# A hybrid network on one core: twelve logarithms of ScalarE moved behind the second head's copies

## What is computed

```python
sim = k @ q_i                                   # causal: -inf beyond query i
_, top_idx = jax.lax.top_k(sim, 8)              # eight keys
for comb in COMBS:                              # all singles, then all pairs of the eight slots
    idx = concat([i], top_idx[slots])           # the query's own key and one or two others
    K = k[idx]; V = v[idx]
    gram = einsum('cnd,cmd->cnm', K, K)
    det = jnp.linalg.det(gram)
    log_det = jnp.log(jnp.where(valid, det, 1.0) + 1e-06)
    score = log_det / float(s + 1)
    w = softmax(einsum('cnd,d->cn', K, q_i) / 4)
    out_s = einsum('cn,cnd->cd', w, V)
probs = softmax(scores)
y = probs @ outs
```

## Time and profile before

| | us |
|---|---|
| median of 3 runs | 6697.57 |
| lowest, highest | 6695.38, 6705.53 |
| profiled execution, its own time | 6691.49 |
| its span, first to last instruction | 6689.8 |

### The profile page before, as it was taken

The page is one execution under the profiler, slowest core; times in us unless marked ns, Lnnn a source line. Parts: engine busy times, 40 slices in busy tenths (PEclk is TensorE's granted clock), DMA queues, the critical chain, the costliest instruction groups (busy, mean ns, idle before and its releaser), DMA issues. The chain is left out here.

```text
span 6689.8 us, 140956 instructions
## 1 busy us (share of the span) xinstructions
PE 4900.3 (73%) x46216; PEld 3823.2 (57%) x46217; DVE 4611.5 (69%) x9872; ACT 2738.6 (41%) x9313; POOL 1463.5 (22%) x1253
## 2 busy tenths in 40 slices
PE   5777776867877777777877788765089498419995
PEld 2333334756666666666666666655078376419995
DVE  5777774328999999999999999994168744312224
ACT  3343342214555555555555555542322133333331
POOL 1323322110000000000000000000645200266663
PEclk8777778987667777767767777765599699559997
DMA  8000000002111111211211111111222500211114
GB/s 144 8 5 7 5 3 6 0 7 78 71 68 70 72 65 72 72 69 69 72 72 66 72 71 66 72 59 29 70 70 75 109 0 10 77 61 46 46 46 138
DMA packets 226734, 370.27 MB, mean 55 GB/s; under 512 B 104818, under 2 KB 187355, under 8 KB 201028
## 3 DMA queue, kind: packets, MB, share of 16 engines
q1 hardware_dynamic: 200036, 309.26, 15.6%
q0 software_dynamic: 26112, 53.64, 2.4%
HBM read 287.04 MB, written 75.78 MB: 54 GB/s over the span
## 5 line engine op out<-in xcount | busy, mean ns | idle before, releaser
L2729 PE MATMUL l2a_g<-l2a_feat,l2a_onehot 128*128 128x33 bf16 x27648 | 782.7, 182 | 357.8 <-DVE l2a_onehot L2600 155.6
L2729 PEld LDWEIGHTS l2a_g<-l2a_feat,l2a_onehot 128*128 128x128 bf16 x27648 | 762.1, 100 | 419.0 <-issue 238.7
L2592 DVE TENSOR_REDUCE l2a_dots<-l2a_prod 128x144 f32<-128x2304 f32 x192 | 489.7, 2551 | 4.5
L1942 PE MATMUL l_y<-l_hc,l_selT 128*96 128x512 f32 x384 | 295.4, 864 | 264.9 <-POOL l_hc L1780 264.3
L2675 PE MATMUL l2a_s<-l2a_qkT 32*128 32x128 f32 (+1 forms) x1536 | 488.2, 453 | 0.0
L2701 PE MATMUL l2a_m<-main_ident,l2a_pv 128*96 128x128 f32 x2304 | 349.6, 326 | 87.7 <-DVEq L2537 87.7
L2365 POOL TENSOR_TENSOR l2a_veto<-l2a_gone 128x288 f32<-128x288 f32 x64 | 42.6, 665 | 1681.5 <-DVE l2a_prod L2585 1681.5
L2600 DVE TENSOR_SCALAR l2a_onehot<-l2a_spread,l2a_pos 128x4096 bf16<-128x4096 bf16 x288 | 361.3, 1283 | 62.3 <-DVE l2a_hd L2498 20.1
L2701 PEld LDWEIGHTS l2a_m<-main_ident,l2a_pv 128*96 128x96 f32 x2304 | 341.6, 207 | 103.5 <-issue 100.2
L1780 POOL TENSOR_TENSOR l_hc<-l_hs,l_bc 128x512 f32<-128x512 f32 x192 | 243.3, 1267 | 716.0 <-DVE l_hs L1847 714.8
L2675 PEld LDWEIGHTS l2a_s<-l2a_qkT 32*128 32x128 f32 x1536 | 310.8, 250 | 86.4 <-issue 38.6
(11 more groups left out here) (412 smaller groups left out, 11615.4 us busy)
## 6 DMA issues: line engine op xcount, KB each, us to landing
l2a_spread<-l2a_idx_rows SPq DMA_DIRECT2D x192, 1024.0 KB, 4.7
rows_in<-main_zeros SPq DMA_DIRECT2D x1, 13824.0 KB, 80.3
l2f_xg<-rows_in SPq DMA_DIRECT2D x72, 192.0 KB
l3f_xg<-rows_in SPq DMA_DIRECT2D x72, 192.0 KB, 2.5
l2f_combine_y<-rows_out SPq DMA_DIRECT2D x32, 384.0 KB, 3.8
l3f_combine_y<-rows_out SPq DMA_DIRECT2D x32, 384.0 KB, 4.7
l3f_w<-in_l3f_w SPq DMA_DIRECT2D x2, 4608.0 KB, 31.6
l_xT<-in_l_xT SPq DMA_DIRECT2D x16, 384.0 KB, 3.8
```

The costliest lines, as they stand in the source:

```text
L1942: nc.tensor.matmul(y_ps[:, :], selT[:, g, :], hc[:, g % 2, :], start=g == 0, stop=g == G - 1).then_inc(hc_used, 1)
L2592: nc.vector.tensor_reduce(dots[:, quad_of(s[2]), 0:NPROD], prod[:, :, :, :], AX.X, ALU.add).then_inc(S["dots_ready"], 1)
L2729: ins = nc.tensor.matmul(o[:, a * FEAT:a * FEAT + 2 * HS + 1], onehot[:, kt, at:at + P], feat3[:, s[1], kt, part, h, 0:2 * HS + 1], start= ...
```

## The change

In ScalarE's `body`, `log_det` no longer stands first. In steps with copies it is called inside the loop over the four heads, behind the copies of the second one (j = 1). Where no copies are due (the drain's last step) it stands where it stood. Nothing else is changed, and line numbers behind it move by 2 (L2315 becomes L2313, L2324 becomes L2326).

```diff
--- before.py
+++ after.py
@@ -2298,8 +2298,6 @@
                 def body(n, u, i, back, last):
                     if i == 0 and u == 1:
                         keep_tables()
-                    if stage(back, LOGS):
-                        log_det(*stage(back, LOGS))
                     s = back(2)
                     if s:
                         q, t = count_of(s), s[2] // QUADS
@@ -2316,6 +2314,10 @@
                             nc.scalar.copy(keys[:, s[2] % 2, j, SLOTS:EXT, :], src[:, 0:EXT - SLOTS, 0:HS])
                             ins = nc.scalar.copy(values[:, t, h, :, :], src[:, :, HS:2 * HS + 1])
                             ins.then_inc(S["kv_ready"], 1)
+                            if j == 1 and stage(back, LOGS):
+                                log_det(*stage(back, LOGS))
+                    elif stage(back, LOGS):
+                        log_det(*stage(back, LOGS))
                     if in_range(n):
                         q = count_of((n, u, i))
                         act.wait_ge(S["scored"], counted(q * 2 + 2))
```

## The result

The changed kernel takes 6743.97 us (median of 4 runs, 6741.58 to 6748.62) against 6696.70 us of the kernel before in the same comparison: a ratio of 1.0069, with a 95% interval of 1.0051 to 1.0086. It is slower by 47 us. The forecast was 6717, or 19.5 us slower, with a range to 6734. The direction was right, but the forecast rise was less than half of the measured one, and the time lies outside the range.

What follows compares the result with a forecast made beforehand. VectorE was taken to set the pace; 23.5 us of added waits for the logarithms less a 4 us gain made 19.5 us, so 6717 us from the median 6697.6. The range was 6698 to 6734.

Steps and rivals of the forecast that it cites:

- What bounds the kernel: In the edited stage VectorE sets the pace, busy 379 of 400 us; TensorE, busy 315, does not.
- the third rival: TensorE sets the pace, so some 60 pauses of 3 us come off, 180 us, giving 6518; chance 0.03.
- Step 3, the logarithms: On ScalarE in step 3, the logarithms start 1.2 us later, behind two heads' copies.
- What VectorE pays, the odd images: At L2494: 13 late places (already waiting) pay 1.2 us more each; touching (slack about 0) 1.17; middle (0.19 to 0.43) the uncovered rest.
- What VectorE pays, the even images: At L2494 in step 3: touching places pay 1.17 us each, middle ones 1.2 less their slack, early ones nothing.
- Early: 9 x 0: Nine early step-3 places, all in even images, cost nothing, since a slack of 1.24 us covers the 1.2 us shift.
- Step 0: Logarithms 0.4 us later in even images, 0.7 in odd; slack of 2.19 or more covers it, costing VectorE nothing.
- Early images turn middle or late: If TensorE's clock falls less well, nine early slacks shrink to 0.4 or 0: 7 to 11 us more; chance 0.12.
- TensorE's pauses count: Same as the third rival: TensorE sets the pace and 180 us of pauses come off, giving 6518; chance 0.03.
- Step 3, the copies: TensorE's pause moves to the wait for ScalarE's cast; its next step is 0.3 us later, costing nothing.
- The small gain: In step 4, GpSimd's squares slow VectorE less in late images: 0.26 us each, some 4 us off.
- What would show it: L2494's waits for logarithms some 38 us in 20 or more waits, about 2.3 us each in late images.

Runs made afterwards that it cites:

- e1: The kernel before, with the logarithms moved behind the second head's copies in step 3 alone: 6704.79 us against 6696.87, ratio 1.0015.
- e2: The kernel before, with the logarithms moved behind the second head's copies in step 0 alone: 6698.50 us, ratio 1.0004.
- e3: The changed kernel, with TensorE's fourth head of step 0's gather held until the logarithms are done: 6714.70 us against 6696.87, ratio 1.0026.

## Why the prediction was wrong in size

*What bounds the kernel: right.* VectorE's work fell, its waits for the logarithms rose by 47.2 us, and the stage by 40.7. Over the twelve kernels VectorE's busy time in the stage stays between 2796 and 2810 us, while its idle time goes from 149 to 212. TensorE's 137.7 us of pauses for copied values went, and brought nothing, as the third rival's chance of 0.03 had it.

*Step 3, the logarithms: right.* The shift was to be 1.2 us and is 1.2.

*What VectorE pays, the odd images: the number came, in part by luck.* Thirteen late, one touching, one middle, at 1.1 + 1.2, 1.17 and about 1.0 make 32 us; the odd images of after wait 32.5. But the forecast ascribed this to step 3's move by itself, and with that alone (e1) they wait 20.1, 6 us more than before and not 18, since their fronts come 0.8 us earlier there, which the forecast didn't have.

*What VectorE pays, the even images: this term failed.* "Early: 9 x 0", with what the two touching and four middle ones in even images pay, made 5.7 us; the even images wait 28.3. The 9 x 0 was right for step 3's move by itself (e1: 1.4 us over all even images). It was wrong once the other half of the change was in.

*Step 0: the step that failed.* "Nothing on VectorE waits for it: nothing." The direct part held: the logarithms of step 0 are 0.4 us later in even images and 0.9 in odd ones (forecast 0.4 and 0.7), and the least slack left there is 0.94. The text had TensorE's fourth head 3 us earlier, which is what came. It then looked only for direct waits. The effect goes a longer way: no pause, an earlier TensorE, a longer wait for one-hot rows, a stall in the next gather, the clock left at 0.50 (which of these lowers it is open), scores and fronts 1.8 us longer, L2224 later, and with it the logarithms of step 3, which VectorE does wait for. Step 0's move was priced against step 0's slack of 2.19 us, when it had to be priced against step 3's, 1.24 in the same image, of which step 3's own move had already spent 1.2. By itself step 0's move takes 0.6 us of slack from the even images (0.85 to 0.23 in the mean, e2); on top of step 3's move it takes 1.95 (0.06 in e1 to -1.89 in after).

*The rival that came true was under-priced.* "Early images turn middle or late" named the mechanism, TensorE's clock, and gave it 0.12 and 7 to 11 us. It let the slacks shrink to 0.4 or 0 and stopped there. They went to -1.9 in the mean, and all 15 even images, not 9, were hit. The bound should have come from the rows: an image at the lower clock is late by what its scores and fronts take longer, and the odd images, whose fronts come late, stood as the example, with slacks near -1.1. Even images made like the late odd ones would have cost 15 x 2.3 = 35 us where the sum had 6: 29 more, 6746.

*The rival that TensorE's pauses count:* its small chance was right, its price was off. It took 60 pauses of 3 us, 180 us, where the earlier trace rows have 137.7 us in 61. That changes nothing in the sum.

*Step 3, the copies:* the pause was moved to the cast, as forecast, up to 4.1 us long. The transpose of step 3 starts 6.26 us behind L2224's start in the even image of after, 6.03 in the early image of before (both shown above): 0.2 us later, forecast 0.3. That cost nothing that the waits show.

*The small gain: about right.* Forecast 4 us, VectorE's busy time fell by 6.8. GpSimd's squares still lie beside these VectorE rows, but begin earlier in them: L2518 (L2516 before) now takes 919 ns at most instead of 1212, L2524 (L2522) 454 instead of 820, and L2517 (L2515) 1298 instead of 1028. Summed up, L2517, L2518 and L2523 to L2525 take some 3 us less; the rest of the 6.8 is elsewhere.

*What would show it.* The waits for the logarithms were to be 38 us in 20 or more; they are 61.8 in 30. The wait of late images was to be 2.3, and is 2.32 in the odd image shown.

## What to carry to other kernels

An edit that lets an engine off the critical path stop waiting is not free because nothing waits for it there: its work and its clock move, and what it delivers two steps later may be the thing that the pacing engine has least slack for. When one change spends slack in two places, follow both to the same wait before asking whether the slack covers them, and test them together: here the halves spent 0.8 and 0.6 us and the whole 2.7. And before moving work later on a shared in-order engine, look at what it stands behind: here the copies ahead of the logarithms were the cause of the waits, and moving those gave 0.27%.

## What the runs showed of the hardware

- TensorE got slower by being given less waiting. With a 3.00 us pause in step 0 the clock in and behind the next gather was 0.89 and 0.68; without it 0.50 and 0.50. Fourteen unread matmuls of 1.67 us together brought it back to 0.93, and took 26.9 us off VectorE's waits. The pause alone doesn't decide it: with only step 0's half of the change in (e2) the pause is gone too, and the clock is 0.78 and 0.50.
- The low clock costs its time with or without a stall: from transpose to transpose 16.93 us at 0.94 and 0.63 with a stall of 0.86 us, 18.49 at 0.74 and 0.55 with none (e3).
- A gather of 192 matmuls, fed and unhindered, can stand still for 0.8 to 1.6 us with nothing to wait for that the profile shows. It does so behind the 116th matmul in all 15 even images of after, and in one of before.
- The same program's untouched layers were 12.9 us apart between the two profiled executions. For an edit of this size, the stage's own length and VectorE's idle time in it (+40.7 and +47.4) say more than the span (+53.6).
